# Degree counts from 32 full-width products, with 14 staircase columns and one weight split moved to GpSimd

## What is computed

```python
def _gcn(x, src, dst, W, b, n):
    deg = segment_sum(ones_like(src), dst, num_segments=n)   # self-loops included
    dinv = where(deg > 0, deg ** (-0.5), 0.0)
    norm = dinv[src] * dinv[dst]
    h = x @ W
    return segment_sum(h[src] * norm[:, None], dst, num_segments=n) + b

h = maximum(layernorm(x), 0)
h = batchnorm(h) * bn_w + bn_b
h = _gcn(h, src, dst, gcn_in_w, gcn_in_b, n)
```

## Time and profile before

| | before |
|---|---|
| median of 3 runs | 2465.84 us (2465.4 to 2469.6) |
| the profiled execution | 2466.82 us |
| its span, first to last instruction | 2464.9 us |
| mean granted TensorE clock | 0.99 |
| busy: PE, DVE, ACT, POOL | 97%, 67%, 46%, 28% |

### The profile page before, as it was taken

One profiled execution on the slowest core, in us unless ns is written; L12 is line 12 of the kernel. 1 busy time (PEld: TensorE's weight loads), 2 busy tenths in 40 slices (PEclk: granted clock), 3 DMA queues, 4 the chain that ended last, 5 costly groups with the idle time before them and its releaser, 6 DMA issues.

```text
span 2464.9 us, 37083 instructions
## 1 busy us (share of the span) xinstructions
PE 2397.8 (97%) x12215; PEld 1987.6 (81%) x12215; DVE 1658.9 (67%) x3202; ACT 1133.3 (46%) x2280; POOL 687.4 (28%) x521
## 2 busy tenths in 40 slices
PE   6879999999999999999999999999999999999999
PEld 5448888878888888878888888878888888878887
DVE  8896776766655776665565676665566677665666
ACT  8974344554334344554334334554334434644332
POOL 3000000156631000156541000066540000066541
PEclk8989999999999999999999999999999999999999
DMA  2021100112221100112211100122211100022122
GB/s 77 1 88 54 35 17 34 35 52 69 69 64 44 35 34 17 35 52 75 70 64 37 35 34 18 35 65 73 66 59 35 35 34 26 27 73 73 60 75 101
DMA packets 82646, 122.44 MB, mean 50 GB/s; under 512 B 5808, under 2 KB 63536, under 8 KB 77872
## 3 DMA queue, kind: packets, MB, share of 16 engines
q1 hardware_dynamic: 82480, 120.32, 14.7%
HBM read 116.10 MB, written 4.19 MB: 49 GB/s over the span
## 4 chain that ended last, share of the span: by engine, by line
PE 83%; DVE 7%; issue 4%; POOL 3%; ACT 2%; DMA 0%; DVEq 0%; POOLq 0%; SPq 0%; ACTq 0%
PE ps L1871 17%; PE ps L1872 17%; PE ps L1873 17%; PE ps L2190 7%; PE ps L2192 7%; PE ps L2194 7%; PE ps L2112 2%; PE ps L2129 2%; PE ps L2131 2%; DVE oh_d L1382 1%; PE ps L2126 1%; PE ps L1993 1%; PE ps L1994 1%; POOL f_lo L632 1%; PE ps L1927 1%
## 5 line engine op out<-in xcount | busy, mean ns | idle before, releaser
L550 POOL TENSOR_SCALAR veps<-mv 128x1 f32<-128x1 f32 x65 | 17.3, 266 | 1005.6 <-DVE mv L1176 1005.6
L1808 DVE TENSOR_TENSOR h<-h,ps 128x512 f32<-128x512 f32 x256 | 170.2, 684 | 74.5 <-PE ps L1873 74.5
L632 POOL TENSOR_TENSOR f_lo<-ff,f_hi 128x512 fp32r<-128x512 f32 x128 | 166.4, 1310 | 177.7 <-ACT f_hi L1062 177.7
L1871 PE MATMUL ps<-cond_hi,w_hi 128*128 128x512 f32 x512 | 203.6, 398 | 0.0
L1871 PE MATMUL ps<-w_hi,cond_hi 128*128 128x512 f32 x512 | 200.9, 392 | 0.6 <-POOL w_lo L557 0.3
L1872 PE MATMUL ps<-cond_lo,w_hi 128*128 128x512 f32 x512 | 200.0, 391 | 0.0
L1873 PE MATMUL ps<-w_hi,cond_lo 128*128 128x512 f32 x512 | 200.0, 391 | 0.0
L1873 PE MATMUL ps<-cond_hi,w_lo 128*128 128x512 f32 x512 | 200.0, 391 | 0.0
L2190 PE MATMUL ps<-xT_hi,wg_hi 128*128 128x512 f32 x480 | 187.9, 391 | 12.4 <-POOL wg_lo L659 12.4
L1872 PE MATMUL ps<-w_lo,cond_hi 128*128 128x512 f32 x512 | 199.7, 390 | 0.0
L1871 PE MATMUL ps<-wf_hi,f_hi 128*128 128x512 f32 x512 | 199.2, 389 | 0.0
(11 more groups left out here) (308 smaller groups left out, 6701.1 us busy)
## 6 DMA issues: line engine op xcount, KB each, us to landing
stage<-in_pieces SPq DMA_DIRECT2D x82, 512.0 KB, 3.3
stage<-in_condT SPq DMA_DIRECT2D x33, 1024.0 KB, 4.8
stage<-in_pieces SPq DMA_DIRECT2D x224, 128.0 KB, 2.6
x<-in_x SPq DMA_DIRECT2D x2, 1024.0 KB, 6.5
at_s<-at SPq DMA_DIRECT2D x1, 2048.0 KB, 6.2
at16b<-at_s SPq DMA_DIRECT2D x1, 2048.0 KB, 10.1
out<-h SPq DMA_DIRECT2D x8, 256.0 KB, 2.0
bias_row<-in_rows SPq DMA_DIRECT2D x6, 256.0 KB, 3.3
```

The source lines that it names most:

```text
L632: pool.tensor_tensor(f_lo[q % 2][:, c, half * HALF:(half + 1) * HALF], ff[:, s % 2, :], bits(f_hi[q % 2][:, c, half * HALF:(half + 1) * HA ...
L1808: dve.tensor_tensor(h[:, t, :], h[:, t, :], ps[:, down_bank(q, t), :], ALU.add)\
L1871: pe.matmul(bank, l_hi, r_hi, start=(first and i == 0), stop=False)
```

## The change

GpSimd subtracts 14 of the 32 staircase columns (18 to 31), right behind `x_nm` of the second half, and a new VectorE step `high_reached` compares them with 0, between `batch_stats(1)` and the scatters of chunks 8 to 15. ScalarE's `d_apart(18, 32)` goes. These columns then hold 1 and 0 in place of +1 and -1, which `stairs` makes up for. The weight split of piece 1 goes from VectorE to GpSimd, behind those columns and ahead of the wait for the batch statistics. TensorE takes four columns of edges per product: 32 products of 128 by 128, of which only the blocks on the diagonal count. VectorE gathers these four blocks (into `full`), adds them, and corrects the 14 columns.

```diff
--- before.py
+++ after.py
@@ -78,6 +78,7 @@
 
     HEAVY, PICKS = 1024.0, 32
     G_FIRST, G_STEP = 15, 14
+    SIGNS = 18
     DIGIT, MID_LOW, MID_HIGH = 5776.0, 2880.0, 2880.0
     SHIFT, MINUS = 545.0, -238.5
     ROUND = 1.5 * 2.0 ** 23
@@ -576,6 +577,11 @@
                 if half == 0:
                     w_low(0, 0, attn_place(0, 0, 0), attn_place(1, 0, 0))
 
+            pool.tensor_tensor(d_high[:, SIGNS:, :], d5[:, 1, :].unsqueeze(1).broadcast_to([P, 32 - SIGNS, CHUNKS]),
+                               iota0[:, SIGNS:32].unsqueeze(2).broadcast_to([P, 32 - SIGNS, CHUNKS]),
+                               ALU.subtract).then_inc(d_low_ok, 1)
+            w_low(1, 1, attn_place(0, 0, 1), attn_place(1, 0, 1))
+
             pool.wait_ge(b_ln, 2 * KC)
             pool.tensor_scalar(x_veps[:, 0:KC], x_mv[:, 0:KC, 1], EPS, None, ALU.add).then_inc(b_rs, 1)
             pool.wait_ge(b_rs, 1)
@@ -734,7 +740,7 @@
 
             act.wait_ge(d5_ok, 1)
             act.wait_ge(steps_ok, 1)
-            d_apart(0, 18)
+            d_apart(0, SIGNS)
 
             def z1_of(t):
                 act.wait_ge(x_rs, 4)
@@ -789,7 +795,6 @@
                 x0T_of(t)
             for t in range(4, NT):
                 x0T_of(t)
-            d_apart(18, 32)
             signs(8, G_FIRST + 1)
             for k in range(KC):
                 if k >= 2:
@@ -1296,6 +1301,10 @@
                 dve.wait_ge(d_low_ok, 1)
                 dve.tensor_scalar(d_low[:, :, :], d_low[:, :, :], 0.0, None, ALU.is_equal).then_inc(d_oh_ok, 1)
 
+            def high_reached():
+                dve.wait_ge(d_low_ok, 2)
+                dve.tensor_scalar(d_high[:, SIGNS:, :], d_high[:, SIGNS:, :], 0.0, None, ALU.is_ge).then_inc(d_oh_ok, 1)
+
             def y_of(k):
                 dve.wait_ge(bn_ok, 3)
                 dve.tensor_scalar(y_place(k), x0T[:, k, :], bn[:, k:k + 1], bn[:, KC + k:KC + k + 1], ALU.mult, ALU.add)\
@@ -1322,23 +1331,33 @@
             low_equal()
             batch_stats(0)
             batch_stats(1)
+            high_reached()
             scatters(8, G_FIRST + 1)
             batch_scale()
             for k in range(2):
                 y_of(k)
             for k in range(2):
                 y_low(k)
-            dve.wait_ge(w_ok, 1)
-            first_w_low(1)
             for k in range(2, KC):
                 y_low(k)
             for c in range(G_FIRST + 1, CHUNKS):
                 scatter(c)
                 if c == G_FIRST + 6:
                     dve.wait_ge(deg_mm, 1)
-                    dve.tensor_scalar(stairs[0:32, 0:32], ps[0:32, 2, 0:32], 0.5, None, ALU.mult).then_inc(stairs_ok, 1)
-                    dve.tensor_scalar(stairs[0:32, 32:33], ps[0:32, 2, 0:1], -0.5, None, ALU.mult).then_inc(stairs_ok, 1)
+                    for e in range(4):
+                        last = dve.tensor_scalar(
+                            full[0:32, 0, 32 * e:32 * e + 32],
+                            ps[32 * e:32 * e + 32, 2, 0:P].rearrange("p (v e) -> p v e", e=4)[:, :, e], 0.5, None, ALU.mult)
+                    last.then_inc(stairs_ok, 1)
+                    dve.wait_ge(stairs_ok, 1)
+                    dve.tensor_reduce(stairs[0:32, 0:32], full[0:32, 0, 0:P].rearrange("p (e v) -> p v e", e=4), AX.X,
+                                      ALU.add).then_inc(stairs_ok, 1)
                     dve.wait_ge(stairs_ok, 2)
+                    dve.tensor_scalar(stairs[0:32, 32:33], stairs[0:32, 0:1], -1.0, None, ALU.mult).then_inc(stairs_ok, 1)
+                    dve.wait_ge(stairs_ok, 3)
+                    dve.tensor_scalar(stairs[0:32, SIGNS:32], stairs[0:32, SIGNS:32], 2.0, stairs[0:32, 32:33],
+                                      ALU.mult, ALU.add).then_inc(stairs_ok, 1)
+                    dve.wait_ge(stairs_ok, 4)
                     for q in range(4):
                         last = dve.scalar_tensor_tensor(deg[32 * q:32 * q + 32, :], stairs[0:32, q:32:4], 1.0,
                                                         stairs[0:32, q + 1:33:4], ALU.add, ALU.subtract)
@@ -1931,11 +1950,12 @@
                     for t in range(4, NT):
                         x_transpose(t)
                 if c == G_FIRST:
-                    pe.wait_ge(d_oh_ok, 1)
-                    pe.wait_ge(d_apart_ok, 2)
-                    for e in range(CHUNKS):
-                        last = pe.matmul(ps[0:32, 2, 0:32], d_low[:, e, :], d_high[:, :, e], start=(e == 0),
-                                         stop=(e == CHUNKS - 1))
+                    pe.wait_ge(d_oh_ok, 2)
+                    pe.wait_ge(d_apart_ok, 1)
+                    for e in range(0, CHUNKS, 4):
+                        last = pe.matmul(ps[:, 2, 0:P].rearrange("p (v e) -> p v e", e=4),
+                                         d_low[:, e:e + 4, :].rearrange("p e n -> p (e n)"), d_high[:, :, e:e + 4],
+                                         start=(e == 0), stop=(e == CHUNKS - 4))
                     last.then_inc(deg_mm, 1)
                 if c == 48:
                     pe.wait_ge(ge_ok, 1)
```

## The result

The changed kernel takes 2473.23 us (median of 11 runs, 2470.65 to 2475.00), the one before 2466.61 us beside it on the same chip (11 runs, 2465.03 to 2469.60). The ratio is 1.0026, with a 95% interval of 1.0017 to 1.0034: slower by 6.6 us by the medians and by 5.9 us by the means. The profiled execution of the change took 2471.78 us, its span is 2469.9 us against 2464.9.

The account below looks back on a forecast made before the run. A chain through GpSimd's x_nm, VectorE and ScalarE to the first g_product bounds the early part: 5.0 (held tiles) + 0.5 (compare) = +5.5 us, 2472.3 profiled, 2471.3 as median; range 2467.0 to 2473.5.

Parts of the forecast that it names:

- the forecast mechanism: First 50 us: held z1 tiles plus the added compare give +5.5 us, 2470.0 to 2472.5; chance 0.50.
- The two GpSimd operations (+5.0): Behind x_nm: digit columns and weight split hold VectorE's z1 tiles, so the d_low compare ends 5.0 us later.
- The order of turns: VectorE z1 tiles: one turn per GpSimd instruction; columns end at 24.1, split at 26.6, d_low compare at 29.0.
- C: VectorE's z1 tiles: GpSimd doesn't hold them, only the compare costs, +0.5, 2466.3 us; chance 0.12.
- C': VectorE's z1 tiles: only one of the two GpSimd operations costs, +3.0, 2468.8 us; chance 0.08.
- The high compare (+0.5): VectorE, between statistics and scatters: the added high_reached lengthens the chain by 0.5 us.
- The parts worth 0 up to g: Before the first g_product: removed ScalarE columns, removed VectorE split, wide products and longer staircase each worth 0.
- Rival B (the clock): First g_product: dense products wake TensorE's clock, 2.5 us gained, 2468.8 us; chance 0.15.
- The step that failed: Behind the first g_product: no load or timed event, so a shift of its 40.02 us start shifts the end.

Follow-up runs that it names:

- products-alone kernel: The kernel before plus only the 32 wide products and the longer staircase; ratio 1.0006, median 2.1 us above before.
- off the chain: The changed kernel with GpSimd's two operations waiting for the last z1 tile and both compares between pieces of y; ratio 0.9999, median 0.4 us below before.

## Why the prediction was right, and where it wasn't

*Direction and size.* 2471.3 us was forecast, as 5.5 us above the 2465.8 of three runs; 2473.23 was measured, 6.6 us above the 2466.6 of eleven. So of the 1.9 us between forecast and measurement 0.8 lie in the base and 1.1 in the change. The measured time is inside the whole range, but only by 0.3 us at its upper end, and outside the 2470.0 to 2472.5 that the forecast mechanism had for itself. That it still fell in is luck: the range was that wide for other rivals, and what filled it stood in none of them. Slower by more than 0.2% had 0.49, and that is what came by the ratio of 1.0026, whose interval begins at 1.0017.

*The two GpSimd operations (+5.0).* Right in mechanism and size. Statistics start 4.86 us later (28.86 for 24.00). The order of turns was as worked out: the digit operation ends at 24.04 (24.1 forecast), the split at 26.53 (26.6), the low compare at 28.86 (29.0). Rivals C and C' fall with tiles of 3.33 us, and with the split put back: each operation held one tile. The section of the Trainium skill's page SBUF — State Buffer, "Who interferes with whom", that the prediction drew on agrees with all of it, the kernels with the memset and with z1 on ScalarE among them, and so does its other side: statistics, beside the same GpSimd operations, kept 0.68 us. Tile 4 ended 0.28 us after its GpSimd instruction, as in the earlier trace rows.

*The high compare (+0.5).* 0.49 us in the chain. Right.

*The parts worth 0 up to g.* All right, and the products-alone kernel shows it: g at 40.17. Sizes were off where it didn't matter: the 32 products took 77 ns each where the prediction had them between 106 (3.4 us) and 232 ns (7.4 us), because the clock rose while they ran (off the chain, all at 0.50, they took 112 ns); ScalarE waited 4.39 us ahead of the first yT_hi, not 5.5, because its copies of x0T came later too (the last ended at 30.3), with its one-hots behind them; the staircase's extra came to 1.35 us for 1.1.

*Rival B (the clock).* Half true: the clock did rise, while the wide products ran. Stretches of the changed kernel around them:

```profile
36.90:39.40 2.50, 2.48 (x34) 2.31 (x32) 2.45 (x4) 2.29 (x3) 0.00 (x0) 0.79 0.04 7
39.40:42.00 2.60, 0.00 (x0) 0.00 (x0) 1.67 (x3) 2.60 (x4) 0.00 (x0) 0.88 0.00 0
42.00:45.00 3.00, 0.00 (x0) 0.00 (x0) 1.96 (x2) 3.00 (x6) 0.00 (x0) 0.50 0.00 0
45.00:48.00 3.00, 2.60 (x6) 2.12 (x7) 2.89 (x12) 1.41 (x5) 0.00 (x0) 0.50 0.00 0
```

In finer stretches the clock is 0.50 until 37.9, when TensorE had been busy for 2.9 us with 16 chunk products and about a dozen of the wide ones, 1.00 from 38.4 to 41.0, and 0.50 again from 41.5, in the idle time that the prediction had named against B. That the wide form alone does it is not shown. Off the chain, behind 5.50 us of idle time, the same products ran wholly at 0.50:

```profile
36.66 3.59 PE L1957 MATMUL ps<-d_high,d_low 128*128 128x128 f16 x32 [5.50 <-DVE d_high L1307]
```

There the clock rose only behind 41, inside the first g_product (0.50 over 40 to 41, 0.69 over 41 to 42), and g2 came 1.9 us earlier than before with g at the same place. Before, it stood at 0.50 through the small products and the whole first g_product.

*The step that failed.* "Everything behind is fed by this product, in a chain without a load or a timed event in it, so a shift of 40.02 is a shift of the end." That is false: the layers hold loads, and weight splits behind them, that can end later than TensorE needs them. Already in before TensorE waits in the layers for such splits, 0.3 us once for w_lo and 3.1 us in each layer for wg_lo. And removing 96 products was priced only by their time on TensorE; that it shortens the program ahead of the loop of the layers stood in no row that I read. The six kernels of that length were 1.3 to 3.5 us later than their g2 said, the seven others 0.2 to 0.7; the same code with its length given back was 1.4 to 2.4 us faster. So of the 6.6 us of the medians some 4.8 to 5.4 are the held tiles and the compare, and 1.2 to 1.8 are the layers (0.9 by the means).

What stays open: whether the fetch as such delays the load or only comes with it; and why the clock loss near 386 us is missing in some layers and doubled in others, behind the same wait of 3.1 us. Before with a shorter TensorE program and nothing else changed wasn't run.

## What to carry to other kernels

Work given to an idle GpSimd is free only if VectorE has no compare, scaling or two-operand step from SBUF to SBUF in those microseconds: each GpSimd instruction held one such step for its whole length, so place it beside statistics, or behind the chain. When a change removes or adds many instructions ahead of a loop, look at the instruction queue's packets and at the waits in the loop, and build a twin of the same length before the difference is put down to the work removed.

## What the runs showed of the hardware beyond that

- A GpSimd memset, which reads nothing, holds a VectorE tile like an operation with two operands: 2842 ns for 542 beside a memset of 2.66 us.
- The hold goes both ways: x_nm on GpSimd took 1.47 us in place of 0.31 while VectorE's compare ran, which kept its 1.21 us.
- In the change the granted clock rose from 0.50 to 1.00 inside 32 products of 128 by 128 in 16 bits that followed 16 chunk products without a gap. Off the chain, behind 5.50 us of idle time, the same 32 ran at 0.50 to their end, and so did 128 products of 128 by 32 with TensorE 100% busy before.
- One more instruction packet of some 16 KB in that stretch of a layer goes with a weight load whose reader starts 0.4 to 0.9 us later (three pairs of kernels), and, in this kernel, with 1.7 to 2.8 us of waits for w_lo over three layers.
